# Moving a second bias from the last stage of a mixture-of-experts layer into its routing, and cutting the last stage into six pieces

## What is computed

```python
logits = xt @ Wg.T
topk_logits, topk_idx = jax.lax.top_k(logits, 2)
w = jax.nn.softmax(topk_logits, axis=-1)
gates = zeros((T, 8)).at[rows, topk_idx].add(w)
h = gelu(einsum('th,ehi->tei', xt, W1) + b1)
o = einsum('tei,eih->teh', h, W2) + b2
y = einsum('te,teh->th', gates, o)
x = layernorm(x + y)
```

## Time and profile before

| | |
|---|---|
| median of 3 runs | 709.72 us (704.99 to 710.05) |
| span of the profiled execution | 709.1 us |
| routing | 421 to 456 us |
| experts | 456 to 672 us |
| last part | 672 to 709 us |

### The profile page before, as it was taken

The page is one execution under the profiler, slowest core; times in us unless marked ns, Lnnn a source line. Parts: engine busy times, 40 slices in busy tenths (PEclk is TensorE's granted clock), DMA queues, the critical chain, the costliest instruction groups (busy, mean ns, idle before and its releaser), DMA issues. The chain is left out here.

```text
span 709.1 us, 13416 instructions
## 1 busy us (share of the span) xinstructions
PE 597.9 (84%) x5136; PEld 406.7 (57%) x5136; DVE 536.7 (76%) x978; ACT 404.1 (57%) x603; POOL 322.1 (45%) x359
## 2 busy tenths in 40 slices
PE   5989788888999799898987850799999999999950
PEld 2435344353454435444654540598999999998840
DVE  5587575536877588867756759899999999999574
ACT  4555578753466354455651311288788787876534
POOL 9311255444255244525452431435665755761334
PEclk9999899998999899999999995699999999999965
DMA  8306344393001801011030014578888888785173
GB/s 231 133 1 159 81 149 149 118 214 147 1 1 60 221 20 43 18 61 31 1 120 1 1 52 172 173 273 270 299 280 281 283 267 305 235 302 193 48 244 119
DMA packets 71599, 102.04 MB, mean 144 GB/s; under 512 B 4960, under 2 KB 59432, under 8 KB 70512
## 3 DMA queue, kind: packets, MB, share of 16 engines
q1 hardware_dynamic: 67792, 90.96, 40.1%
q0 software_dynamic: 3744, 10.23, 4.4%
HBM read 80.27 MB, written 20.84 MB: 143 GB/s over the span
## 5 line engine op out<-in xcount | busy, mean ns | idle before, releaser
L236 DVE TENSOR_REDUCE rowmax<-M 128x1 f32<-128x512 f32 (+3 forms) x176 | 104.6, 635 | 45.9 <-PE M L226 43.9
L681 ACT ACTIVATE probs<-R 128x1024 f32<-128x1024 f32 x80 | 80.4, 1027 | 59.6 <-PE R L1027 59.2
L209 PE MATMUL HB<-xT,w 128*128 128x256 f16 (+1 forms) x1104 | 107.1, 257 | 0.0
L1757 PE MATMUL YB<-w,h 128*128 128x256 f16 x936 | 105.9, 273 | 0.1
L209 PEld LDWEIGHTS HB<-xT,w 128*128 128x128 f16 x1104 | 94.9, 98 | 9.8 <-DVE xT L1610 0.6
L1757 PEld LDWEIGHTS YB<-w,h 128*128 128x128 f16 x936 | 91.5, 98 | 10.7 <-issue 0.4
L543 POOL TENSOR_SCALAR_AFFINE_SELECT probs<-probs 128x256 f32<-128x256 f32 x128 | 49.7, 407 | 104.1 <-ACT probs L681 103.3
L1453 ACT ACTIVATE hf<-HB,b 128x256 f32<-128x256 f32 (+1 forms) x184 | 70.4, 443 | 44.7 <-PE HB L209 42.6
L1349 POOL DMA_INDIRECT xg<-scratch_xs,src x39 | 77.2, 1979 | 26.0 <-issue 11.0
L1357 POOL DMA_INDIRECT scratch_ys<-y,dst x39 | 43.5, 1115 | 81.8 <-ACT y L1433 76.4
L1622 DVE SCALAR_TENSOR_TENSOR w<-w2f,w 128x2048 f16<-128x2048 f32 x23 | 52.6, 2285 | 9.3 <-ACT w L1439 9.3
(11 more groups left out here) (256 smaller groups left out, 1052.3 us busy)
## 6 DMA issues: line engine op xcount, KB each, us to landing
w1f<-in_W SPq DMA_DIRECT2D x23, 1024.0 KB
w2f<-in_W SPq DMA_DIRECT2D x23, 1024.0 KB
scratch_ax<-stage SPq DMA_DIRECT2D x16, 256.0 KB, 2.5
scratch_vw<-stage SPq DMA_DIRECT2D x16, 256.0 KB, 2.8
vw<-scratch_vw SPq DMA_DIRECT2D x4, 1024.0 KB, 5.6
a_x<-scratch_ax SPq DMA_DIRECT2D x4, 1024.0 KB, 7.0
parts<-scratch_ys SPq DMA_DIRECT2D x8, 512.0 KB, 7.4
scratch_qk<-qk SPq DMA_DIRECT2D x6, 512.0 KB, 3.9
```

Of the source, the lines that this page charges most:

```text
L209: last = nc.tensor.matmul(out, left(a, k), right(b, k), start=(k == 0 and m == 0), stop=(k == n - 1 and m == 2))
L236: return nc.vector.tensor_reduce(rowmax[:, t, par * PAIRS + p0:par * PAIRS + p0 + pairs], bank[:, 0:pairs * wide].rearrange("p (n w) -> p ...
L681: A.activation(probs[:, n % RING, :, :], bank[:, :, :], ACT.Exp, scale=1.0 / (QS * QS)).then_inc(empty, 1)
L1757: last = M.matmul(YB[q][:, t, :], h[:, q, a, m, t * 128:t * 128 + 128], w2[:, q, b, m, :], start=((m, a, b) == (0, 0, 0)), stop=((m, a) == ...
```

## The change

The second bias is made in the routing: DVE makes `gate` before it reads PE's count, POOL makes `share` right after, PE does its 16 transposes and 16 calls of the product with `b2` between the count and the `slot_map` matmuls, and ACT copies the eight results from PSUM into `parts[:, :, 0, :]`, before it turns to the first weights. PE may not issue its first thrown-away matmul before these copies are done, since it writes a bank that they read. During the experts POOL adds one tile of the bias to `z` between gather n and scatter n - 4, for n = 4 to 19. SP starts the loads of `parts` once all 16 are added.

The last part goes in six pieces of 2, 2, 4, 4, 2 and 2 tiles. In the first two pieces, and for two of the four tiles of the next two, DVE alone weighs and adds the second output; for the other eight tiles ACT weighs and POOL adds, as before. ACT's order is now: weigh piece 2, normalize piece 0, weigh 3, normalize 1, weigh 4, normalize 2, weigh 5, normalize 3, normalize 4. POOL's part of `root` is two steps; DVE makes `shift` of piece k after the statistics of piece k + 1, and it normalizes the last piece itself.

The diff, cut to its core:

```diff
+LAST = [(0, 2), (2, 4), (4, 8), (8, 12), (12, 14), (14, 16)]
+ALONE_IN_LAST = [2, 2, 2, 2, 0, 0]
...
+    def bias_bank(j):
+        return (YB[1], HB[2], XBS[0], XBS[1], HB[0], HB[1], YB[1], HB[2])[j]
... (SP)
+        sp.wait_ge(bias_added, NT)
+        for k, (a, b) in enumerate(LAST):
...
... (POOL)
         pool.wait_ge(consts, 8)
+        pool.wait_ge(gate_done, 1)
+        for c in range(2):
+            P.tensor_tensor(share[:, c, :, :], hot[:, c, :, :], gate[:, c, :].unsqueeze(2).to_broadcast([128, NT, NE]),
+                            ALU.mult).then_inc(share_step, 1)
+        pool.wait_ge(share_step, 2)
+        P.tensor_tensor(share[:, 0, :, :], share[:, 0, :, :], share[:, 1, :, :], ALU.add).then_inc(share_done, 1)
         pool.wait_ge(halves_found, 1)
...
         for n in range(4, TILES):
             gather(n)
+            if n - 4 < NT:
+                pool.wait_ge(bias_out, (n - 4) // 2 + 1)
+                P.tensor_tensor(z[:, n - 4, :], z[:, n - 4, :], parts[:, n - 4, 0, :], ALU.add).then_inc(bias_added, 1)
             scatter(n - 4)
...
+        weighed = 0
+        for k, (a, b) in enumerate(LAST):
+            first = a + ALONE_IN_LAST[k]
+            if first < b:
+                weighed += 1
+                pool.wait_ge(part_done, weighed)
+                P.tensor_tensor(z[:, first:b, :], z[:, first:b, :], parts[:, first:b, 1, :], ALU.add
+                                ).then_inc(pairs_added, 1)
+            if k >= 1:
+                root(k - 1)
+        root(len(LAST) - 1)
... (ACT)
+        for k in range(NT // NQ):
+            act.wait_ge(turn_full, k + 1)
+            A.activation(shareT[:, k, :], turned(k), ACT.Copy).then_inc(turn_done, 1)
+        for j in range(NT // 2):
+            act.wait_ge(bias_full, j + 1)
+            A.activation(parts[:, 2 * j:2 * j + 2, 0, :], bias_bank(j)[:, :, :], ACT.Copy).then_inc(bias_out, 1)
...
+        weigh(0)
+        weigh(1)
+        for k, (a, b) in enumerate(LAST[:-1]):
+            if k + 2 < len(LAST):
+                weigh(k + 2)
+            act.wait_ge(shift_done, k + 1)
+            for t in range(a, b):
+                last = A.activation(z[:, t, :], z[:, t, :], ACT.Identity, bias=shift[:, t:t + 1],
+                                    scale=rstd[:, t:t + 1])
             last.then_inc(z_done, 1)
... (DVE)
+        pairs = 0
+        for k, (a, b) in enumerate(LAST):
+            own = a + ALONE_IN_LAST[k]
+            dve.wait_ge(parts_in[k], 2 * 16)
+            for t in range(a, own):
+                last = V.scalar_tensor_tensor(z[:, t, :], parts[:, t, 1, :], gate[:, 1, t:t + 1], z[:, t, :],
+                                              ALU.mult, ALU.add)
...
+            if k > 0:
+                shifted(k - 1)
+        a, b = LAST[-1]
+        dve.wait_ge(root_done, len(LAST))
+        dve.wait_ge(z_done, len(LAST) - 1)
+        for t in range(a, b):
+            last = V.tensor_scalar(z[:, t, :], z[:, t, :], meanvar[:, t, 0:1], rstd[:, t:t + 1],
+                                   ALU.subtract, ALU.mult)
+        last.then_inc(z_done, 1)
... (PE, behind rank and total)
+        pe.wait_ge(share_done, 1)
+        for k in range(NT // NQ):
+            for t in range(NQ):
+                last = M.transpose(turned(k)[:, t * 128:t * 128 + 128], share[:, 0, k * NQ + t, :], ident[:, :])
+            last.then_inc(turn_full, 1)
+        pe.wait_ge(b2_in, 16)
+        for j in range(NT // 2):
+            pe.wait_ge(turn_done, min(max(j // 2 + 1, j - 1), NT // NQ))
+            if j >= 6:
+                pe.wait_ge(bias_out, j - 5)
+            for t in range(2 * j, 2 * j + 2):
+                last = M.matmul(bias_bank(j)[:, t % 2, :], shareT[:, t // NQ, t % NQ * 128:t % NQ * 128 + 128], b2[:, :],
+                                start=True, stop=True)
+            last.then_inc(bias_full, 1)
...
             last = M.matmul(slot_map, in_row[:, i, :], in_half[:, :, i, :], start=i == 0, stop=i == 2 * NT - 1)
+            if i == NT // 2:
+                pe.wait_ge(bias_out, NT // 2)
             if NT // 2 <= i < 2 * NT - 1:
                 keep_running(1, 1)
```

More of the change, by code:

```diff
@@ L1363, in _ @@
             gather(n)
[L1364 to L1369, removed]
         pool.wait_ge(dst_done, 1)
@@ L1474, in weigh @@
         def weigh(k):
[L1476 to L1485, removed]
-            last.then_inc(z_done, 1)
[L1489 to L1495, removed]
+            a, b = LAST[k]
+            if a + ALONE_IN_LAST[k] < b:
+                act.wait_ge(parts_in[k], 2 * 16)
+                for t in range(a + ALONE_IN_LAST[k], b):
+                    last = A.activation(parts[:, t, 1, :], parts[:, t, 1, :], ACT.Copy, scale=gate[:, 1, t:t + 1])
+                last.then_inc(part_done, 1)
+        weigh(0)
[7 more added lines that the diff above has]
+                                    scale=rstd[:, t:t + 1])
+            last.then_inc(z_done, 1)
     @block.vector
@@ L1531, in _ @@
         V.tensor_tensor(hot16[:, :, :], hot[:, 0, :, :], hot[:, 1, :, :], ALU.add).then_inc(hot_done, 1)
[L1532 to L1533 removed]
+        dve.wait_ge(gexp_done, 1)
+        after(V.tensor_scalar(gap[:, :], gate[:, 1, :], 1.0, None, ALU.add))
+        after(V.reciprocal(gate[:, 0, :], gap[:, :]))
+        V.tensor_tensor(gate[:, 1, :], gate[:, 1, :], gate[:, 0, :], ALU.mult).then_inc(gate_done, 1)
         dve.wait_ge(ranks, 1)
@@ L1652, in _, with shifted @@
             step(n, n // 2, n % 2)
[L1654 to L1668, removed]
-                dve.wait_ge(parts_in[k], 2 * 16)
-                for t in tiles:
-                    last = V.scalar_tensor_tensor(z[:, t, :], parts[:, t, 1, :], gate[:, 1, t:t + 1], z[:, t, :],
-                                                  ALU.mult, ALU.add)
+        def shifted(k):
+            a, b = LAST[k]
+            dve.wait_ge(root_done, k + 1)
+            V.scalar_tensor_tensor(shift[:, a:b], meanvar[:, a:b, 0], -1.0, rstd[:, a:b], ALU.mult, ALU.mult
+                                   ).then_inc(shift_done, 1)
+        pairs = 0
+        for k, (a, b) in enumerate(LAST):
+            own = a + ALONE_IN_LAST[k]
[3 more added lines that the diff above has]
+                                              ALU.mult, ALU.add)
+            if own > a:
                 after(last)
-            else:
-                dve.wait_ge(part_added, k)
-            for t in tiles:
+            if own < b:
+                pairs += 1
+                dve.wait_ge(pairs_added, pairs)
+            for t in range(a, b):
                 last = V.scalar_tensor_tensor(z[:, t, :], parts[:, t, 0, :], gate[:, 0, t:t + 1], z[:, t, :],
```

92 lines of the change are left out of this document (29 added, 63 removed).

## The result

The kernel with the change is slower: median 725.09 us (721.27 to 728.14, four runs) against 707.48 us of the kernel before, run beside it (704.99 to 710.05, four runs). The ratio is 1.0226, with a 95% interval of 1.0185 to 1.0266. The forecast was 713.0 us, with a range to 718.0; the time lies outside it.

What follows compares the result with a forecast made beforehand. It took small DVE instructions to bound the routing, PE the experts, and a chain over several engines the last part. Routing +4.8, experts +0.5 and last part -1.4 gave +3.9 on 709.1, so 713.0 us; range 707.0 to 718.0.

Steps and rivals of the forecast that it cites:

- The routing, +4.8 us: Routing: PE's bias work at clock 0.50 delays the end of the map from 448.97 to 453.8; bounds +0.1 and +6.
- the weakest step: Routing: a clock that falls under the bias work also won't rise under it, so products take 0.427 us each.
- The gate instructions, cost nothing to move: Routing: making gate before DVE reads PE's count costs the chain only 0.1 us, with gate ready at 429.9.
- The experts, +0.5 us: Experts: POOL's 16 additions delay DVE, but its idle time nearly covers this; +0.5 us, bounds 0 and +3.
- The price of an addition: Experts: each POOL addition costs DVE 0.6 us, between 0 and 0.73; 9.6 us for 16.
- The cover: Experts: DVE's 8 to 9 us idle over 160 us plus 1.8 us of lead absorb the additions' 9.6 us on average.
- DVE falls behind in the experts: Experts: rival that additions cost more than DVE's idle time absorbs, +4 instead of +0.5, total 716.5; chance 0.18.
- the sign written down for it: Experts: PE idle time released by DVE's `w` or `h` would show that DVE falls behind; no size given.
- The last part, -1.4 us: Last part: earlier final normalization gives -1.0 and a smaller last store -0.4; bounds -4.5 and 0.
- additions of POOL that hold DVE up by 1.4 us: Last part: upper bound of its term, where POOL's additions delay DVE by 1.4 us and the gain is 0.
- the DVE case: Experts: rival that each addition costs DVE more than its idle time absorbs, +4, total 716.5; chance 0.18.
- the own case: Whole kernel: the author's main forecast, 710 to 716 with its own bounds, experts up to +3; chance 0.55.

Runs made afterwards that it cites:

- e4: The changed kernel plus three useless small DVE copies before DVE's first low part of the weights; median 723.21 us, ratio 1.0162 to the kernel before.
- e6: Apparently (label not spelled out) the changed kernel with the 16 bias additions moved from POOL to DVE, behind the experts; median 719.06 us, ratio 1.0146.
- e7: Apparently (label not spelled out) the changed kernel with ACT weighing pieces 4 and 5 one place earlier; 721.33 us, ratio 1.0189.
- e3: The changed kernel with thrown-away matmuls before the count, before the bias transposes and between the bias products; median 731.63 us, ratio 1.0320.
- e9: The kernel before with 11 more thrown-away matmuls between map and first gathered rows, and DVE normalizing the last piece; median 710.10 us, ratio 1.0004.

## Why the prediction was wrong

**The routing, +4.8 us: right.** The window from 430 to 442 is at 0.50, eight products take 3.41 us, 0.427 each as forecast, the last ends near 447.8 (forecast 448.9) and the map ends at 452.6 (453.8). From R the way to it is 4.8 us longer, as the sum had it. That it fits to a tenth is partly luck: with the same code up to the map, e4, e6 and e7 took 33.3 us instead of 32.6. There the clock was at 0.50 from R on and the count came 0.7 us later; in the kernel after it was at 1.00 for the first 1.5 us. That the work which let the clock fall in the last part wouldn't raise it in the routing was called the weakest step. It held, and so did the stronger form in e3.

**The gate instructions, cost nothing to move: wrong, 1.6 us.** The text priced the new place, 0.1 us, and left out what stood behind the old one. That was DVE's first low part, and a start 0.6 us sooner brought it into the issue of the first gather. Shown by e4.

**The experts, +0.5 us: this is the step that failed; it measured +7.6.** The step read: "9.6 against 8.5 + 1.8 just fits on average, not at each place", and took the average. Two terms were mis-sized.
The price of an addition was taken as 0.6 us of DVE, from one conversion beside `share`; it measured 0.88. It was bounded above by POOL's own 0.73 us. That bound doesn't hold: an addition that is itself held up reaches into a second DVE instruction.
The cover was the larger error in kind. DVE's idle time was summed over 160 us, and the tightest place was said to have 1.8 us of lead, at the low part of W2. But PE also waits for `xT`, and there the kernel before has next to nothing:

```profile
518.46 0.68 DVE L1610 SCALAR_TENSOR_TENSOR xT<-XB,xT 128x512 f16<-128x512 f32 x1
519.26 1.30 PEld L209 LDWEIGHTS HB<-xT,w 128*128 128x128 f16 x12
```

DVE ends at 519.14 and PE loads at 519.26: 0.1 us, and so, or less, it is at eight of the 23 `xT` of the kernel before. What delays DVE in the microseconds before delays PE. All five waits of the kernel after are for `xT`. They make 6.1 of the 7.2 us that the additions cost; where the other 1.1 us is, the waits don't show. The rival "DVE falls behind in the experts" had this mechanism, at +4; it was the right case and too small, and the sign written down for it, PE idle behind `w` or `h`, named the wrong operands. The rule of the Trainium skill (SBUF — State Buffer, "Who interferes with whom"), priced at the whole 0.73 us of each addition, was nearer than my 0.6 and still short of 0.88; with the cover as I had it, it gave +1.4. Nor is it only the later instruction that is held, as the prediction had it from there: DVE's at 517.32 had started 0.6 us ahead of POOL's and took 2.88 us all the same. Even the right price would have given 14.1 - 10.3 = +3.8. The rest is the cover: it took up 6.9 of the 14.1 us and not 10.3, which leaves the 7.2 us. (Another 0.4 us the experts take longer with the fills too, 217.1 against 216.7.)

**The last part, -1.4 us: wrong, +1.8.** The mechanism stands: ACT weighs the last two tiles at 711.69, right behind the normalization of piece 2, and DVE waits for them:

```profile
711.69 0.89 ACT L1487 ACTIVATE parts<-parts,gate 128x256 f32<-128x256 f32 x2
...
714.03 0.88 DVE L1678 SCALAR_TENSOR_TENSOR x_all<-parts,gate,x_all 128x256 f32<-128x256 f32 x2 [2.44 <-POOL x_all L1396]
```

Against the last product (the end of the experts, 685.2 here) three sizes were off. Piece 2 was in 13.1 us behind it, not 11.7 as the eighth tile before: the same bytes in twelve issues over 9.3 us instead of eight over 7.0. Whether the number of issues is the cause was not tried. One collision with POOL cost 1.0 us:

```profile
705.06 2.71 DVE L1678 SCALAR_TENSOR_TENSOR x_all<-parts,gate,x_all 128x256 f32<-128x256 f32 x4
...
706.24 1.26 POOL L1396 TENSOR_TENSOR x_all<-x_all,parts 128x512 f32<-128x512 f32 x1 [0.33 <-ACT parts L1487]
```

I had priced this as a bound ("additions of POOL that hold DVE up by 1.4 us"), and taken nothing. Together these put the last normalization at 32.8 us behind the last product, where 31.2 was forecast. And from its end to the end of the span it is 5.7 us, not 4.2: a store of 256 KB lands in 2.2 us at the median against 2.9 for 512 KB, but the last two stores are issued 0.85 us apart. The bytes are not the cause: DMA stops at 719.8, and the span ends 3.9 us later, against 2.0 before. In e9, with the last two stores of 512 KB 2.2 us apart instead of 3.4, it is 2.7. That points at stores that follow each other closely, but it was not tried.

**The range** ended at 718.0, since the DVE case had been given +4 with an upper bound for the own case of +3. Both came from the same idea of a cover, so the range was no protection against that idea being wrong.

## What to carry to other kernels

A POOL instruction that reads SBUF isn't free because POOL is idle: price it as DVE time, here at somewhat more than its own length, and look for the place where another engine waits for DVE with no lead, not at DVE's idle share. When small instructions are moved away from an engine, look at what then starts sooner and beside what. Small matmuls in a place at the lower clock were made cheap here by work put ahead of them, not by work between them.

## What the runs showed of the hardware

- A POOL issue of an indirect gather took 1.22 us when DVE's 128x2048 operation with two SBUF inputs started 0.4 us behind it, and 3.18 us when that started 0.2 us ahead. Beside DVE's additions of two SBUF tiles a scatter's issue took 1.50 us instead of 0.97.
- A DVE instruction of 0.13 us took 1.15 us beside a POOL addition, so a short one can lose as much as a long one (1.0 us against 1.1 for four additions). Statistics with one SBUF input kept their 1.40 us beside the same kind of addition; conversions with one SBUF input grew, from 0.42 to 0.94 us (128x512) and from 0.29 to 0.82 (128x256).
- Fills by POOL (341 ns each) changed no DVE duration by more than 2 ns against the kernel before in the two-input forms (2286 against 2285 ns, 694 against 692).
- With 8 rows of weights and PE busy throughout, the clock fell from 1.00 to 0.50 even with a matmul of 512 columns and 128 rows between every two token tiles of the product.
